# Theta and phi on two column tiles of 64, a quarter of the tokens in each

## What is computed

```python
theta = (einsum('bhwc,cd->bhwd', x, w_theta) + b_theta)        # (b, 1024, 32)
phi = maxpool2x2(einsum('bhwc,cd->bhwd', x, w_phi) + b_phi)    # (b, 256, 32)
g = maxpool2x2(einsum('bhwc,cd->bhwd', x, w_g) + b_g)          # (b, 256, 128)
attn = softmax(einsum('bnd,bmd->bnm', theta, phi))
out = einsum('bhwd,dc->bhwc', attn @ g, w_o) + b_o
return x + out * sigma
```

## Time and profile before

| | us |
|---|---|
| median of three timed runs | 526.87 |
| lowest and highest of them | 522.64, 527.66 |
| profiled execution, its own time | 524.93 |
| its span | 523.1 |
| PE busy | 456.5 (87% of the span) |
| DVE busy | 286.2 (55%) |
| ACT busy | 211.7 (40%) |
| POOL busy | 120.6 (23%) |

### The profile page before, as it was taken

The page is one execution under the profiler, slowest core; times in us unless marked ns, Lnnn a source line. Parts: engine busy times, 40 slices in busy tenths (PEclk is TensorE's granted clock), DMA queues, the critical chain, the costliest instruction groups (busy, mean ns, idle before and its releaser), DMA issues.

```text
span 523.1 us, 9272 instructions
## 1 busy us (share of the span) xinstructions
PE 456.5 (87%) x3727; PEld 320.2 (61%) x3727; DVE 286.2 (55%) x609; ACT 211.7 (40%) x336; POOL 120.6 (23%) x163
## 2 busy tenths in 40 slices
PE   0978988978599999998999999989989897988966
PEld 0956755645357666665687676656766574665734
DVE  3619433855555437847863375457546737537253
ACT  1112110555134333675416145655346474463340
POOL 5601200176001200375102000681012021100000
PEclk9998888999798999999999999999989998899989
DMA  7492885785804790157026920293117310000112
GB/s 209 92 207 43 187 127 104 127 197 70 117 0 59 101 235 7 59 90 111 9 82 101 184 34 2 82 121 63 43 42 102 62 42 1 2 3 1 41 41 82
DMA packets 30489, 42.90 MB, mean 82 GB/s; under 512 B 6075, under 2 KB 21230, under 8 KB 30446
## 3 DMA queue, kind: packets, MB, share of 16 engines
q1 hardware_dynamic: 23886, 35.08, 37.0%
q0 software_dynamic: 3584, 4.50, 3.2%
q10 hardware_dynamic: 2976, 2.73, 2.7%
HBM read 16.16 MB, written 4.19 MB: 39 GB/s over the span
## 4 chain that ended last, share of the span: by engine, by line
PE 64%; DVE 11%; DMA 8%; POOL 5%; issue 5%; ACT 5%; SPq 0%; ACTq 0%; DVEq 0%; POOLq 0%
PE ps_d L735 8%; PE ps_d L723 5%; PE ps_d L860 5%; PE ps_d L755 5%; PE ps_d L837 5%; PE ps_d L937 5%; PE ps_s L784 4%; PE ps_v L826 4%; PE ps_t L803 4%; PE ps_v L820 4%; DMA q_st<-mx_t 3%; PE ps_d L879 2%; DMA xa<-in_x_dram 2%; DVE mx L1560 2%; POOL samp L1871 2%
## 5 line engine op out<-in xcount | busy, mean ns | idle before, releaser
L1189 ACT ACTIVATE prob<-ps_t 128x1024 f32<-128x1024 f32 x64 | 65.4, 1022 | 102.3 <-PE ps_t L803 101.4
L1560 DVE TENSOR_REDUCE mx<-ps_s 128x4 f32<-128x1024 f32 x64 | 78.2, 1222 | 34.4 <-PE ps_s L784 33.3
L1843 POOL DMA_DIRECT2D q_st<-mx_t x64 | 34.1, 534 | 261.2 <-ACT mx_t L1181 244.8
L735 PE MATMUL ps_d<-cstack,conv_w 128*32 128x256 f32 x1024 | 59.9, 388 | 3.5 <-DMA cstack<-qpad 3.1
L784 PE MATMUL ps_s<-k_st,q_st 96*128 96x256 f32 x256 | 51.4, 325 | 8.5 <-DVE mx L1560 5.6
L803 PE MATMUL ps_t<-q_st,k_st 98*128 98x256 f32 x256 | 43.9, 295 | 12.7 <-DMA q_st<-mx_t 6.1
L735 PEld LDWEIGHTS ps_d<-cstack,conv_w 128*32 128x32 f32 x1024 | 35.7, 110 | 25.3 <-issue 6.2
L784 PEld LDWEIGHTS ps_s<-k_st,q_st 96*128 96x128 f32 x256 | 37.3, 198 | 21.7 <-DVE mx L1560 9.6
L803 PEld LDWEIGHTS ps_t<-q_st,k_st 98*128 98x128 f32 x256 | 36.7, 198 | 15.4 <-issue 7.7
L820 PE MATMUL ps_v<-prob,vh 128*32 128x256 f32 x512 | 36.2, 402 | 0.8 <-DVE att L1574 0.7
L1574 DVE TENSOR_TENSOR att<-ps_v,rden 128x256 f32<-128x256 f32 x32 | 13.6, 424 | 40.3 <-ACT rden L1200 40.2
(11 more groups left out here) (177 smaller groups left out, 751.0 us busy)
## 6 DMA issues: line engine op xcount, KB each, us to landing
q_st<-q_parts SPq DMA_DIRECT2D x42, 256.0 KB, 6.8
xa<-in_x_dram SPq DMA_DIRECT2D x8, 512.0 KB, 9.0
z_all<-in_x_dram SPq DMA_DIRECT2D x8, 512.0 KB, 9.2
out_dram<-z_all SPq DMA_DIRECT2D x8, 512.0 KB, 2.6
cstack<-qpad SPq DMA_DIRECT2D x22, 180.5 KB, 5.7
k_st<-cstack SPq DMA_DIRECT2D x24, 128.0 KB, 3.9
q_st<-z_all SPq DMA_DIRECT2D x6, 256.0 KB, 5.6
cstack<-att SPq DMA_DIRECT2D x6, 180.5 KB, 6.0
```

The source lines that it names most:

```text
L735: ins = pe.matmul(ps[32 * k:32 * k + 32, 0, :], conv_w[:, cb * 4 + k, y, x, :], cstack[:, cb, k, y:y + HG_, x:x + WG_], start=n == 0, stop ...
L1189: drain(act.activation(prob[:, u % 2, 2 * pr:2 * pr + 2].rearrange("p h m s -> p (h m) s"), ps_t[:], ACT.Exp), t_ring, "t", b, u, pr)
L1560: drain(dve.tensor_reduce(mx[:, u % 2, half, :], ps_s[:], AX.X, ALU.max), s_ring, "s", b, u, half)
```

## The change

`w_tp` holds w_theta and w_phi once, 64 columns. TensorE's new `theta_phi` makes four matmuls of 64 columns and 256 tokens: for each half of the channels one for each quarter of the image (`qt`), the first into partitions 0 to 63, the second into 64 to 127 of the same bank, columns 0 to 255. Theta then lies in partitions 0 to 31 and 64 to 95, phi in 32 to 63 and 96 to 127. ScalarE copies each quarter of theta into rows 0 and 2 of the stack, four activations of 32x256; VectorE takes the maximum of phi by two quarters, waits for all four activations, and makes row 1 from the product and the rounded copy, by two quarters. Two of the three loads of w_theta go.

```diff
@@ -238,7 +238,7 @@
         w_vh = sb("w_vh", [P, CB, C])
         mo = sb("mo", [P, CB, C])
         mlp = sb("mlp", [P, CB, C])
-        w_tp = sb("w_tp", [P, CB, 4 * C8])
+        w_tp = sb("w_tp", [P, CB, 2 * C8])
         w_g = sb("w_g", [P, CB, C2])
         w_o = sb("w_o", [P, C])
         bq_all = sb("bq_all", [P, 2, C])
@@ -387,8 +387,8 @@
         ln2_dev = signal("ln2_dev", 2)
         zn_done = signal("zn_done", NT)
         y_done = signal("y_done", 4)
-        th_hi = signal("th_hi", 2)
-        ph_pooled = signal("ph_pooled", 2)
+        th_hi = signal("th_hi", 8)
+        ph_pooled = signal("ph_pooled", 4)
         ph_step = signal("ph_step", 4)
         g_bias = signal("g_bias", 1)
         max1_hi = signal("max1_hi", 1)
@@ -447,9 +447,8 @@
         for_rest.add_to_all_rows(mob_all[:], a["L0_conv_mo_b"])
         for_rest.add_matrix(mlp[:], a["L0_conv_mlp_w"])
         for_image.add_to_all_rows(mlpb_all, a["L0_conv_mlp_b"])
-        for row in range(3):
-            for_rest.add_matrix(w_tp[:, :, row * C8:(row + 1) * C8], a["L1_conv_w_theta"])
-        for_rest.add_matrix(w_tp[:, :, 3 * C8:4 * C8], a["L1_conv_w_phi"])
+        for_rest.add_matrix(w_tp[:, :, 0:C8], a["L1_conv_w_theta"])
+        for_rest.add_matrix(w_tp[:, :, C8:2 * C8], a["L1_conv_w_phi"])
         for_rest.add_matrix(w_g[:], a["L1_conv_w_g"])
         for_rest.add(w_o[:], a["L1_conv_w_o"])
         for_rest.add_to_all_rows(bo_all[:], a["L1_conv_b_o"])
@@ -493,7 +492,11 @@
 
         def by_rows_of(ps):
 
-            return ps.rearrange("p a s -> p (a s)").rearrange("p (q j) -> p j q", j=NJ)
+            return ps.rearrange("p (q j) -> p j q", j=NJ)
+
+        def quarter_of_theta(row, lh, qt):
+            half = th_st[row * C8:(row + 1) * C8, lh * HALF:(lh + 1) * HALF].rearrange("p (j q) -> p j q", j=NJ)
+            return half[:, :, qt * C8 * 2:(qt + 1) * C8 * 2]
 
         def unit_at(u):
 
@@ -879,6 +882,17 @@
                     ins = pe.matmul(ps[:].rearrange("p a s -> p (a s)"), w[:, kt, :],
                                     turned_tile(b)[:, kt, lh * HALF:(lh + 1) * HALF], start=kt == 0, stop=kt == 1)
                 close_bank(ins, dense, name, b, lh)
+
+            def theta_phi(b, lh):
+
+                ps = open_bank(dense, "tp", b, lh)
+                for kt in range(CB):
+                    read_by(dense, "yt", b, lh, kt)
+                    for qt in range(2):
+                        first = lh * HALF + qt * S_
+                        ins = pe.matmul(ps[64 * qt:64 * qt + 64, 0, :], w_tp[:, kt, :],
+                                        turned_tile(b)[:, kt, first:first + S_], start=kt == 0, stop=kt == 1)
+                close_bank(ins, dense, "tp", b, lh)
 
             def scores1(b, lh):
                 if lh == 0:
@@ -979,7 +993,7 @@
                 if s == 3 and post:
                     project(m, 1, 0)
                     project(m, 1, 1)
-                    project1(m, "tp", w_tp, 0)
+                    theta_phi(m, 0)
                 if s == 4 and post:
                     turn_rows(m, 1)
                 if in_front(b, s, "conv0"):
@@ -987,7 +1001,7 @@
                 if in_front(b, s, "conv1") and b == 0:
                     conv(n, conv_halves(n)[1], FIRST_STEPS)
                 if s == 6 and post:
-                    project1(m, "tp", w_tp, 1)
+                    theta_phi(m, 1)
                     project1(m, "g", w_g, 1)
                 if s == 7 and post:
                     max_rows1(m)
@@ -1221,11 +1235,14 @@
 
             def theta_hi(b, lh):
                 ps = await_bank(act, dense, "tp", b, lh)
-                act.activation(th_st[0:3 * C8, lh * HALF:(lh + 1) * HALF].rearrange("p (j q) -> p j q", j=NJ),
-                               by_rows_of(ps[0:3 * C8]), ACT.Identity, bias=bth_c[0:3 * C8]).then_inc(th_hi.sem, 1)
+                for row in (0, 2):
+                    for qt in range(2):
+                        of = slice(2 * C8 * qt, 2 * C8 * qt + C8)
+                        act.activation(quarter_of_theta(row, lh, qt), by_rows_of(ps[of, 0, :]), ACT.Identity,
+                                       bias=bth_c[of]).then_inc(th_hi.sem, 1)
 
             def phi_hi(b):
-                act.wait_ge(ph_pooled.sem, ph_pooled.at(b, 2))
+                act.wait_ge(ph_pooled.sem, ph_pooled.at(b, 4))
                 for row in range(3):
                     act.activation(ph_st[row * C8:(row + 1) * C8], ph_pool, ACT.Identity,
                                    bias=bph_c[2 * C8:3 * C8]).then_inc(ph_step.sem, 1)
@@ -1617,24 +1634,28 @@
             def pooled(src, dst):
                 return dve.tensor_reduce(
                     dst.rearrange("p (y x) -> p y x", x=W // 2),
-                    src.rearrange("p a s -> p (a s)").rearrange("p (y i x k) -> p y x i k", i=2, k=2, x=W // 2),
+                    src.rearrange("p (y i x k) -> p y x i k", i=2, k=2, x=W // 2),
                     AX.XY, ALU.max)
 
             def theta_phi(b, lh):
                 ps = await_bank(dve, dense, "tp", b, lh)
-                pooled(ps[3 * C8:4 * C8], ph_pool[:, lh * P:(lh + 1) * P]).then_inc(ph_pooled.sem, 1)
-                dve.wait_ge(th_hi.sem, th_hi.at(b, lh + 1))
-                mid_rows, n = slice(C8, 2 * C8), slice(lh * HALF, (lh + 1) * HALF)
-                part = th_st[mid_rows, n].rearrange("p (j q) -> p j q", j=NJ)
-                drain(dve.scalar_tensor_tensor(part, by_rows_of(ps[mid_rows]), bth_c[mid_rows], part.bitcast(F32),
-                                               ALU.add, ALU.subtract), dense, "tp", b, lh)
+                for qt in range(2):
+                    pooled(ps[(2 * qt + 1) * C8:(2 * qt + 2) * C8, 0, :],
+                           ph_pool[:, lh * P + qt * 2 * C8:lh * P + (qt + 1) * 2 * C8]).then_inc(ph_pooled.sem, 1)
+                dve.wait_ge(th_hi.sem, th_hi.at(b, 4 * lh + 4))
+                for qt in range(2):
+
+                    of, hi = slice(2 * C8 * qt, 2 * C8 * qt + C8), quarter_of_theta(2 * qt, lh, qt)
+                    ins = dve.scalar_tensor_tensor(quarter_of_theta(1, lh, qt), by_rows_of(ps[of, 0, :]), bth_c[of],
+                                                   hi.bitcast(F32), ALU.add, ALU.subtract)
+                drain(ins, dense, "tp", b, lh)
 
             def g_rows(b, lh):
                 ps = await_bank(dve, dense, "g", b, lh)
-                drain(pooled(ps[:], g_pool[:, lh * P:(lh + 1) * P]), dense, "g", b, lh)
+                drain(pooled(ps[:].rearrange("p a s -> p (a s)"), g_pool[:, lh * P:(lh + 1) * P]), dense, "g", b, lh)
 
             def phi_lo(b):
-                dve.wait_ge(ph_pooled.sem, ph_pooled.at(b, 2))
+                dve.wait_ge(ph_pooled.sem, ph_pooled.at(b, 4))
                 dve.wait_ge(ph_step.sem, ph_step.at(b, 3))
                 lo = ph_st[2 * C8:3 * C8]
                 dve.scalar_tensor_tensor(lo, ph_pool, bph_c[2 * C8:3 * C8], lo.bitcast(F32), ALU.add,
```

## The result

The changed kernel took 535.8 us (median of 5 runs, 532.4 to 538.32) beside 526.87 (522.64 to 529.97): 1.0198 times as long, 95% interval 1.015 to 1.0246. The prediction was 526.0 in a range of 522.2 to 529.7, and the time lies above that range. Ratios leave disturbed runs out, medians are of all runs of an experiment, and the profile of experiment 2 is of a disturbed one, of which only the tail is read.

A forecast was written before the change was run, and what follows sets the result against it. TensorE, with 64% of the chain, was taken to bound the kernel, except where other engines carry it. Terms -1.1 - 0.1 + 0 + 0 + 1.05 + 0.2 = +0.05 us gave 525.0 (profile) or 526.9 (median); named 526.0, range 522.2 to 529.7.

The forecast's parts named there:

- Slower, by the clock: Rival: a longer tail wait drops TensorE's granted clock between 482 and 490 us, +1.7 us a fall; chance 0.25.
- Slot 6, images 0 and 1: 0: Two spots where the chain is POOL's: TensorE's gain becomes waiting and later copies stay covered, 0 us.
- ScalarE's term: At each spot, four theta activations of 32x256 take 1.58 us, 0.91 more than the one before; bounds 0.67 to 1.40 more.
- Half 0: Tail, last image: longer copies and subtractions delay the chain to residual_norm, 1.05 us more (0.8 to 1.55).
- Half 1: Tail, last image: product ends 0.7 us earlier, theta's copies take 0.91 more, 0.2 us more (-0.1 to 0.7).
- Slot 3, image 2: No convolution follows; longer copies eat TensorE's gain but for 0.1 us less (0.3 less to 0.4 more).
- TensorE's term: At a spot between wide neighbours, the product on two tiles of 64 costs 1.18 us instead of 1.72, 0.54 less.
- gain everywhere: Rival: all eight spots give 0.54 us (-4.3), slower copies hidden; 520.6 or 522.5 us, chance 0.12.
- tiles one behind the other: Rival: the two tiles don't run together, 0.35 us added a spot, +4.55 in all; 529.5 to 531.4, chance 0.05.
- The loads: Start of the kernel: two w_theta loads go, priced at 0, with 0.5 us allowed if they slowed `xa`.
- the cheap ends: Sum over all spots of the lowest-cost bounds, written as -1.2 us.
- the dear ends: Sum over all spots of the highest-cost bounds, written as +2.1 us.

The follow-up runs named there:

- experiment 2: Changed kernel with unused unit-matrix transposes issued on TensorE in the tail's waits: 529.6 us, ratio 1.0039 to the kernel before.
- with the clock held: Changed kernel and kernel before, both with unused unit-matrix transposes in TensorE's waits in slot 6, last image's slot 3 and tail: 523.42 and 519.84 us.
- experiment 9: Kernel before with unused unit-matrix transposes in TensorE's waits in every slot 6, slot 3 of the last image and the tail: 519.84 us, ratio 0.9931.
- 5: Changed kernel with unused unit-matrix transposes in TensorE's waits in every slot 6, slot 3 of the last image and the tail: 523.42 us, ratio 0.9975.
- experiment 4: Changed kernel with two of the four theta activations left out, so part of theta is missing from its scores: 529.59 us, ratio 1.008.
- experiment 3: Kernel before with its wide product kept, but output copied, pooled and subtracted by quarters as in the change: 534.69 us, ratio 1.0106.
- 7: Kernel before with the last stage reordered, residual_norm ahead of theta's pooling and subtraction, normalisation ahead of theta's copy: 525.6 us, ratio 0.9995.
- 8: Changed kernel with the last stage reordered, residual_norm ahead of theta's pooling and subtraction, normalisation ahead of theta's copies: 529.05 us, ratio 1.0074.
- experiment 12: Changed kernel with unit-matrix transposes in TensorE's waits and the loops over theta's four copies exchanged, quarter outside, row inside: 522.46 us, ratio 0.9951.

## Why the prediction was wrong

- **The step that failed: the sum has no term for the clock.** Every spot was priced with TensorE at full clock. The clock stood beside the sum as a rival, "Slower, by the clock", with a chance of 0.25 and 1.7 us a fall, for one or two falls. That rival named the place and the test (a fall of the granted clock between 482 and 490 us), and the clock did fall at 487.13; but even with it the range ends at 529.7. The runs show 8.2 us in place of the nothing in the sum: 27.3 us more at half clock, at 0.3 us lost for each. The falls in the tail went on for 6.8 and 13.7 us and not for 3.40, and three came at spots that the prediction had priced at 0 or 0.1. It had priced the fall seen in the earlier trace rows and not asked the same at the other spots, though it said of several that TensorE would wait longer there.
- **"Slot 6, images 0 and 1: 0".** TensorE's gain became waiting, as foreseen, but in front of `scores1` (0.93 to 1.68 us) and not for `samp`, where 0.5 us more had been expected. The cover named, the wait for `samp`, protects against later copies, not against a slower keys' product behind the wait.
- **ScalarE's term was mis-sized.** 1.58 us for four copies was taken from pairs of `cstack` that overlap; they took 1.92, inside the bound of 2.08. The missing 0.34 us make up the tail with the clock held. Half 0, from the `att` product to the turned rows, took 9.83 us in experiment 9 and 11.31 in 5: +1.48, forecast 1.05 + 0.34, and 0.10 for the second subtraction's share of 0.97 against 0.87. Half 1, from there to `scores1`, 17.51 and 18.05: +0.54, forecast 0.2 + 0.34.
- **Slot 3, image 2** was forecast at 0.1 less, at most 0.4 more; with the clock held the slots of b = 3 took 0.6 more. The same 0.34 us at two spots would make that; no run takes the two apart.
- **TensorE's term held.** The product takes 1.08 us as a group, the neighbour behind it begins 1.02 behind its start and takes 0.1 to 0.2 longer. The stretch with slot 3 of b = 1 and 2 gave 1.0 us with the clock held; 1.1 was forecast. Going into tiles of 64 and back cost about what it costs with tiles of 32. Neither of the rivals on TensorE's side (gain everywhere, tiles one behind the other) came.
- **The loads**: no gain shows. The first `exps` began between 87.9 and 94.4 us in the profiles with all four loads and between 92.1 and 94.5 in those with two.
- **A slip in the range.** The cheap ends given at the spots add up to -0.9 us (-1.4 with the 0.5 allowed for the loads) and not to the -1.2 written; the dear ends do give +2.1. Nothing hangs on it.

With the clock held the traces give +1.6 us where the sum says +0.05, which lies within its bounds. The range failed because the clock was a case of its own with a small price, and not a possible cost of every term that lengthens a wait.

## What to carry to other kernels

Where TensorE waits for others, look at each wait that an edit lengthens, and price the clock behind it: here 2.0 us more on the tail's chain took 4.9 us more with them. A shorter product makes the wait behind it longer, so a gain on TensorE in front of a wait was worth nothing here and could cost. Work for TensorE in such waits, useful or not, was worth more here than any part of the edit: 0.7% on the kernel before. Whether a given wait will bring a fall could not be told here from its length alone; filling it and reading the granted clock tells.

## What the hardware showed that I had not expected

- **Short waits on another engine bring falls, but the length of one wait does not decide them.** In front of the tail's turned rows TensorE was idle in one piece for 1.98 us (experiment 4), 2.18 (3), 2.34 (7 and 8) and 2.96 (the changed kernel). Each time the granted clock was 0.50 within 1.2 us of the next product's start, for 3.4 us behind the wait of 2.34 and for 6.8 behind the others, though TensorE was then busy 5.75 of 6.82 us. Against a rule by length stand the 2.04 us of experiment 3 with full clock behind them, the two falls of 3.4 and 13.65 us behind nearly equal waits (the kernel before and experiment 4), and a wait of 1.62 us for `mx` near 381.4 us: it stands in both kernels, and only the kernel before has a fall behind it (383.22). What else decides stays open. The Trainium skill ("TensorE: Matmul & The Clock Gate", "HAM oscillation — how this bites in real kernels") tells of idle gaps behind which the array is slow again, each time anew. The traces agree in kind; here the gaps are synchronisation waits of one engine on another, and filling them brought the clock back to 1.00 over 354 us.
- **In these traces activations of one tile overlap only where both sides stay on the same partitions.** Of the four copies of experiment 3 the second and fourth read and write the same 32 partitions as the one before, and begin 0.36 to 0.37 us behind it; the third changes both and begins 0.47 to 0.48 behind: four in 1.65 us. In the changed kernel the second and fourth write the same partitions and read others; in experiment 12 they read the same and write others. In both all are 0.47 to 0.49 apart: 1.92 us. The chain of experiment 3 shows it as two pairs, that of experiment 12 as four single steps:

```profile
482.80 0.71 ACT th_st L1233 x2
483.51 0.03 issue
483.53 0.83 ACT th_st L1233 x2
```

```profile
478.64 0.46 ACT th_st L1271
479.10 0.03 issue
479.13 0.47 ACT th_st L1271
```

  So in these copies neither side alone is enough, and a layout that puts the quarters of a tile on other partitions than their place in the stack pays 0.27 us a spot for it on ScalarE. The Trainium skill ("ScalarE: Activation LUTs", "What ACT_TABLE_LOAD costs") says that activations behind one another overlap by about 93 ns; the traces agree for the pairs (0.45 less 0.36) and not for the others.
